# Mixture-of-experts slots of 256 and 128 rows in place of 256-row slots only

## What is computed

```
x = x + tanh(g_xattn[0]) * L0_xattn(layernorm(x), ctx, ctx)
x = x + tanh(g_ffn[0])   * L0_ffn(layernorm(x))
x = x + tanh(g_xattn[1]) * L1_xattn(ctx, layernorm(x), mask)
x = x + tanh(g_ffn[1])   * L1_ffn(layernorm(x))

def L1_ffn(x):                     # 4096 x 256, float32
    probs = softmax(x @ gate_w + gate_b)          # 8 experts
    top_w, top_idx = top_k(probs, 2); top_w = top_w / sum(top_w)
    h = silu(x @ w1[e]) * (x @ w3[e])             # 256 -> 1024, for each expert e
    out_e = h @ w2[e]                             # 1024 -> 256
    return sum over e of combine[token, e] * out_e
```

## Time and profile before

| | |
|---|---|
| median of 3 runs | 2118.34 us (2112.92 to 2119.6) |
| the profiled execution | 2116.76 us, span from first to last instruction 2115.0 us |
| PE busy over the span | 1902.5 us (90%) |
| DVE busy | 1563.4 us (74%) |
| ACT busy | 1156.6 us (55%) |
| POOL busy | 921.6 us (44%) |
| mean granted PE clock | 0.954 of 2.4 GHz |

### The profile page before, as it was taken

The page is one execution under the profiler, slowest core; times in us unless marked ns, Lnnn a source line. Parts: engine busy times, 40 slices in busy tenths (PEclk is TensorE's granted clock), DMA queues, the critical chain, the costliest instruction groups (busy, mean ns, idle before and its releaser), DMA issues. The chain is left out here.

```text
span 2115.0 us, 36023 instructions
## 1 busy us (share of the span) xinstructions
PE 1902.5 (90%) x11968; PEld 1329.2 (63%) x11968; DVE 1563.4 (74%) x3233; ACT 1156.6 (55%) x2414; POOL 921.6 (44%) x683
## 2 busy tenths in 40 slices
PE   5899999986669999998999999929999999999998
PEld 2566666665223434343434343419999999999998
DVE  7999999993466677776767778547777777777775
ACT  2356665655335555655555655515555666666663
POOL 6999999981633334352434331112222222222222
PEclk8899999998679999999999999959999999999999
DMA  5222222210425151524242441037666666666661
GB/s 172 111 91 111 88 111 111 84 58 1 112 57 123 31 125 60 112 66 105 78 100 91 89 118 34 31 104 254 223 223 217 217 226 228 226 230 226 220 213 60
DMA packets 140067, 271.47 MB, mean 128 GB/s; under 512 B 13915, under 2 KB 91823, under 8 KB 134066
## 3 DMA queue, kind: packets, MB, share of 16 engines
q1 hardware_dynamic: 128812, 244.55, 37.6%
q0 software_dynamic: 10624, 25.26, 3.2%
q10 hardware_dynamic: 518, 0.27, 0.0%
HBM read 201.96 MB, written 71.39 MB: 129 GB/s over the span
## 5 line engine op out<-in xcount | busy, mean ns | idle before, releaser
L1447 DVE CUSTOM_DVE_ANT_0 x_dump<-x_ps,x_bias_q 128x512 bf16<-128x512 f32 x512 | 353.0, 689 | 103.5 <-PE x_ps L1140 90.4
L1316 ACT ACTIVATE x_PT<-x_ps 128x512 f32<-128x512 f32 x512 | 292.2, 601 | 231.5 <-PE x_ps L1155 228.7
L1929 ACT ACTIVATE X<-m_ps 128x256 f32<-128x256 f32 x312 | 119.1, 382 | 226.0 <-PE m_ps L1866 226.0
L1833 POOL DMA_INDIRECT out_dram<-e_y,e_label x78 | 78.9, 1011 | 362.5 <-DVE e_y L1985 350.6
L1140 PE MATMUL x_ps<-x_KS,x_QS 96*128 96x512 bf16 x512 | 200.7, 393 | 26.2 <-DVE x_mx L1447 25.7
L1154 PE MATMUL x_ps<-x_bias_k,x_ident_b 128*128 128x512 bf16 x512 | 196.8, 384 | 2.2 <-issue 1.1
L1155 PE MATMUL x_ps<-x_QS,x_KS 98*128 98x512 bf16 x512 | 196.5, 384 | 0.0
L1968 DVE TENSOR_TENSOR X<-X,m_ps 128x256 f32<-128x256 f32 x312 | 120.5, 416 | 97.0 <-ACT X L1929 92.5
L1866 PE MATMUL m_ps<-e_x_lo,m_hi 128*128 128x256 f32 x640 | 181.3, 283 | 1.5 <-DVE e_x_lo L1953 1.5
L1866 PE MATMUL m_ps<-e_x_hi,m_hi 128*128 128x256 f32 x640 | 180.9, 283 | 0.0
L1866 PE MATMUL m_ps<-e_x_hi,m_lo 128*128 128x256 f32 x640 | 180.7, 282 | 0.0
(11 more groups left out here) (309 smaller groups left out, 5462.9 us busy)
## 6 DMA issues: line engine op xcount, KB each, us to landing
m_raw<-in_L_ffn_w_dram SPq DMA_DIRECT2D x117, 1024.0 KB, 5.2
expert_in<-a_blank SPq DMA_DIRECT2D x34, 1032.0 KB, 4.3
parts<-x_part SPq DMA_DIRECT2D x24, 512.0 KB, 3.8
m_x<-expert_in SPq DMA_DIRECT2D x39, 258.0 KB, 4.8
next_mask_k<-in_maskT_dram SPq DMA_DIRECT2D x32, 256.0 KB, 2.6
next_mask_q<-in_mask_dram SPq DMA_DIRECT2D x29, 256.0 KB, 2.8
x_KS<-parts SPq DMA_DIRECT2D x16, 384.0 KB, 11.0
x_QS<-parts SPq DMA_DIRECT2D x8, 576.0 KB, 6.4
```

Of the source, the lines that this page charges most:

```text
L1316: act.activation(PT[unit % 2][:, k, :], ps_st[e % 3], ACT.Exp, scale=DH ** -0.5).then_inc(exp_done, 1)
L1447: dve.tensor_tensor_reduce(out=dump[:, :], in0=ps_max[m % 2], in1=bias_q[b % 2][:, q, :], scale=1.0, scalar=NEG, op0=ALU.add, op1=ALU.max, ...
L1929: act.activation(silu[f % 2], ps_h[f % 4][:, 0:BLK], ACT.Silu).then_inc(silu_done, 1)
```

## The change

There are still 39 slots, in another mix: 32 of 256 rows and 7 of 128. The order repeats after 10 slots (`ROUND`), of which the fifth and the tenth (`HALVES`) are small, so slots 4, 9, 14, 19, 24, 29 and 34. An expert's rows are cut into blocks of 256, and a rest of up to 128 rows goes to a small slot; a rest above that to a large one. The table of slots becomes two tables, one for each size, where large slots that are left over take small blocks that found no small slot; working it out takes more instructions.

A small slot loads 129 KB of rows and the same three weight arrays. It has 2 transposes instead of 4; in `hidden` the same 96 matmuls, but with 128 moving columns instead of 256; in `project` 24 matmuls instead of 48; one fetch and one store instead of two; and ACT's and DVE's work on rows is half as wide. Its splitting of weights for the next slot is as before. The slots are written out for slots 0 to 9, for the body of a loop with two turns (10 slots each), and for the last nine.

```diff
+FULL = T * TOPK // BLK
+HALF = NE - 1
+NBLK = FULL + HALF
+ROUND = 10
+HALVES = (4, 9)
...
+def tiles_in(q):
+    return 1 if q % ROUND in HALVES else BT
...
@@ experts: load_rows
-            sp.dma_start(xb[p][:, :, :], xs[bass.ds(at, BLK), :].rearrange("(n p) d -> p n d", p=P)).then_inc(x_in[p], 16)
+            sp.dma_start(xb[p][:, 0:tiles, :], xs[bass.ds(at, tiles * P), :].rearrange("(n p) d -> p n d", p=P)).then_inc(x_in[p], 16)
@@ route, gpsimd
-                pool.iota(starts_i[:, :, :], pattern=[[BLK, NBLK], [0, NE]], base=0, channel_multiplier=0).then_inc(iotas, 1)
+                pool.iota(where_i[:, 0, 0:FULL], pattern=[[BLK, FULL]], base=0, channel_multiplier=0).then_inc(iotas, 1)
+                pool.iota(where_i[:, 0, FULL:], pattern=[[P, HALF]], base=FULL * BLK, channel_multiplier=0).then_inc(iotas, 1)
+                pool.iota(where_i[:, 1, 0:FULL], pattern=[[P, FULL]], base=-FULL * P, channel_multiplier=0).then_inc(iotas, 1)
+                pool.iota(where_i[:, 1, FULL:], pattern=[[P, HALF]], base=0, channel_multiplier=0).then_inc(iotas, 1)
@@ route, vector: 22 instructions in a chain become 36
+                dve.wait_ge(iotas, 4)
+                do(dve.tensor_copy(where[:, :, :], where_i[:, :, :]))
                 do(dve.tensor_tensor(total[:, :], routing.ends_at[0:1, :], routing.region[0:1, :], ALU.subtract))
...
+                do(dve.tensor_tensor(past[:, :, :, :], limit[:, :, :].unsqueeze(3).broadcast_to([1, 2, NBLK, NE]), wide(now), ALU.is_ge))
...
@@ tensor: hidden
-                                mm = three_passes(ps_h[f % 4][:, at:at + BLK],
+                                mm = three_passes(ps_h[f % 4][:, at:at + wide],
                                                   [w[p][n][:, c, f * P:(f + 1) * P] for w in (w_hi, w_lo)],
-                                                  [x_hi[p][:, c, :], x_lo[p][:, c, :]], c == 0, c == KC - 1)
+                                                  [x_hi[p][:, c, 0:wide], x_lo[p][:, c, 0:wide]], c == 0, c == KC - 1)
@@ tensor: project
-                        for n in range(BT):
+                        for n in range(tiles):
...
+                for q in range(ROUND):
+                    hidden(0, q)
+                    turn(0, q + 1)
+                    project(0, q)
+                with pe.Fori(1, ROUNDS) as i:
+                    for q in range(ROUND):
+                        hidden(i, q)
+                        turn(i, q + 1)
+                        project(i, q)
```

More of the change, by code:

```diff
@@ new lines, in _ @@
+                do(dve.tensor_scalar(over[:, :], now[:, 0, NE - 1:NE], float(FULL * BLK), None, ALU.subtract))
+                do(dve.tensor_scalar(more[:, :], over[:, :], 0.0, None, ALU.max))
+                do(dve.tensor_scalar(less[:, :], over[:, :], -0.5, None, ALU.mult))
+                do(dve.tensor_copy(limit[:, 0, :], where[:, 0, :]))
+                do(dve.tensor_scalar(limit[:, 1, :], where[:, 1, :], less[:, 0:1], None, ALU.add))
+                do(dve.tensor_scalar(less[:, :], less[:, :], 0.0, None, ALU.max))
@@ new lines, in _ @@
+                do(dve.tensor_scalar(limit[:, 1, FULL:], where[:, 1, FULL:], less[:, 0:1], more[:, 0:1], ALU.add, ALU.subtract))
+                do(dve.tensor_scalar(weight[:, 0, :], size[:, 0, :], -1.0, None, ALU.mult))
+                do(dve.tensor_tensor(weight[:, 1, 0:NE - 1], size[:, 0, 1:NE], size[:, 0, 0:NE - 1], ALU.subtract))
+                do(dve.tensor_scalar(weight[:, 1, NE - 1:NE], size[:, 0, NE - 1:NE], -1.0, None, ALU.mult))
+                wide = lambda a: a[:, :, :].unsqueeze(2).broadcast_to([1, 2, NBLK, NE])
@@ L1867, in three_passes, with hidden @@
                     return mm
-                def hidden(j, i, p):
+                def hidden(i, q):
+                    j, p, wide = at_slot(i, q), q % 2, tiles_in(q) * P
                     for n in range(2):
@@ L1909, in _ @@
-                hidden(LAST, LAST // 2, 0)
-                project(LAST, LAST // 2, 0)
+                                mm.then_inc(y_ps, BT // tiles)
+                turn(0, 0)
+                for q in range(ROUND):
+                    hidden(0, q)
+                    turn(0, q + 1)
+                    project(0, q)
+                with pe.Fori(1, ROUNDS) as i:
+                    for q in range(ROUND):
+                        hidden(i, q)
+                        turn(i, q + 1)
+                        project(i, q)
@@ L1912, in _, with x_high @@
+                for q in REST:
+                    hidden(ROUNDS, q)
+                    if q + 1 in REST:
+                        turn(ROUNDS, q + 1)
+                    project(ROUNDS, q)
             @block.scalar
             def _(act):
-                def x_high(j, i, p):
-                    act.wait_ge(x_used[p], i + 1)
-                    act.activation(x_hi[p][:, :, :].rearrange("p c n -> p (c n)"), ps_x[p], ACT.Copy).then_inc(x_hi_done, 1)
-                def gated_high(j, k):
+                def x_high(i, q):
+                    p, wide = q % 2, tiles_in(q) * P
+                    act.wait_ge(x_used[p], ROUND // 2 * i + q // 2 + 1)
+                    act.activation(x_hi[p][:, :, 0:wide], ps_x[p].rearrange("p (c n) -> p c n", c=KC)[:, :, 0:wide], ACT.Copy)\
+                        .then_inc(x_hi_done, 1)
@@ L1946, in _ @@
-                hidden(LAST, 0, False)
+                    gated_high(j, FC // 2 - 1, wide)
+                x_high(0, 0)
+                for q in range(ROUND):
+                    hidden(0, q)
+                    x_high(0, q + 1)
+                with act.Fori(1, ROUNDS) as i:
+                    for q in range(ROUND):
+                        hidden(i, q)
+                        x_high(i, q + 1)
+                for q in REST:
+                    hidden(ROUNDS, q, q + 1 in REST)
+                    if q + 1 in REST:
+                        x_high(ROUNDS, q + 1)
@@ L1962, in gate @@
+                def gate(i, q, following=True):
+                    j, p, wide = at_slot(i, q), q % 2, tiles_in(q) * P
                     for k in range(FC // 2):
@@ L2007, in _, with slot @@
-                add_y(LAST, 0)
+                                                 op0=ALU.mult, op1=ALU.add).then_inc(y_left, BT // tiles)
+                def slot(i, q):
+                    gate(i, q)
+                    x_low(i, q + 1)
+                    low_part(dve, at_slot(i, q) + 1, 1 - q % 2, 2)
+                    add_y(i, q)
+                x_low(0, 0)
+                for q in range(ROUND):
+                    slot(0, q)
+                with dve.Fori(1, ROUNDS) as i:
+                    for q in range(ROUND):
+                        slot(i, q)
@@ L2010, in layers @@
+                for q in REST:
+                    if q + 1 in REST:
+                        slot(ROUNDS, q)
+                gate(ROUNDS, len(REST) - 1, False)
+                add_y(ROUNDS, len(REST) - 1)
 def layers(nc, x, ctxT, mask, maskT, g_xattn, g_ffn, L0, F0, L1, M1, out):
```

242 lines of the change are left out of this document (111 added, 131 removed).

## The result

| | before | after |
|---|---|---|
| median | 2119.34 us (2112.92 to 2119.6, 5 runs) | 2101.01 us (2097.69 to 2107.98, 5 runs) |
| the profiled execution | 2116.76 us, span 2115.0 | 2105.28 us, span 2103.5 |
| PE busy | 1902.5 us (90%) | 1879.4 us (89%) |
| start of the routing iota to the end of the span | 715.3 us | 700.5 us |

The changed kernel is faster by 0.7%: the ratio of the times is 0.9928, with a 95% interval of 0.9904 to 0.9952. Forecast were 2100 us, measured 2101.0. A number that comes out so close can still be made of errors that cancel, and here it is: that it lies within 1 us is luck.

The account below looks back on a forecast made before the run. PE was taken to bound every slot. Seven small slots at 3.2 us each (-22.5 us) and the table (+5.1 us) took 2116.8 us to 2099.4, stated as 2100 us; range 2084 to 2108 us, with the fast case.

Parts of the forecast that it names:

- The case of the sum: Whole kernel: the gains and costs of the parts add up as priced, giving 2100 us; chance 72%.
- What bounds the kernel: Experts' slots: PE alone decides, at 17.36 us a slot, until another engine fills the shorter slot.
- Part 1: `project` of a small slot: 24 matmuls fewer save 2.79 us; two fewer transposes save 0.22 us.
- Part 2: `hidden` of a small slot: weight loads bind at 0.114 us a matmul, gaining 0.41 us; ends 0 and 1.1.
- Part 3: Work for the next slot coming late in a small slot: 0.2 us lost, ends 0 and 0.8; no other engine full.
- Part 4: Slot table before the experts: its longer chain, hidden by nothing, costs 5.1 us (4.4 to 6.2).
- Part 5: Loop ends, a store and fetch less in small slots, and the tail: all priced at nothing.
- the fast case: `hidden` of small slots: narrow matmuls pace well below 0.1 us, DVE's 12.1 us bound the slot; 2085 us; chance 12%.
- The slow case: `hidden` of small slots: narrow float32r falls back to the plain price, 0.214 us a matmul; 2165 us; chance 11%.
- a gain handed back: Small slots' neighbours: late row work or weights leave 0.5 us gain a slot instead of 3.2; 2118 us; chance 5%.

Follow-up runs that it names:

- body4: Kernel before the change, with only PE's loop made longer: 9 turns of 4 slots instead of 18 turns of 2; 2117.00 us, ratio 0.9997.
- body6: Kernel before the change, with only PE's loop made longer: 6 turns of 6 slots instead of 18 turns of 2; 2132.77 us, ratio 1.0075.
- bf16 kernel: Changed kernel with both operands of `hidden` in small slots read as bf16, the upper halves of the float32r words; 2113.87 us.

## Why the prediction was right

The sum was 2116.8 - 22.5 + 5.1 = 2099.4 us, so 17.4 us less for the experts. Measured are 14 to 15 less. The case of the sum is the one that came; one of its terms, the loop's return, was wrongly at nothing. By parts:

- **What bounds the kernel**: right. The chain runs over PE in every slot, small or large, and the large ones keep their length (`hidden` 11.39 and 11.31 us).
- **Part 1**: right. Turn and half `project` take 3.30 us, 3.22 were forecast. The gain is 2.71 us instead of 2.79, with 0.21 for the transposes ahead of the slot.
- **Part 2**: the mechanism is right, the load binds; the pace was 0.111 us, between the ends of 0.107 and 0.118, and 0.003 under the value taken. 0.68 us gained, 0.41 forecast. It lies midway between its two neighbours, the transposes' 0.107 and L1203's 0.114. (The "eight matmuls" of L1203 are eight records of four, for a plain f32 matmul has two records here; the pace of a load stays.)
- **Part 3**: right that nothing becomes late. DVE's rows at the end of the small slot (remainders, then `x_low`) answer:

```profile
1516.90 0.99 DVE L2042 TENSOR_TENSOR e_g_lo<-X,e_g_hi 128x256 fp32r<-128x256 f32 x2
...
1517.95 0.69 DVE L2017 TENSOR_TENSOR e_x_lo<-m_ps,e_x_hi 128x512 fp32r<-128x512 f32 x1
```

  `x_low` ends at 1518.64, 0.6 us ahead of the next `hidden` at 1519.23, where the prediction had 0.4; the stall that it allowed, 0.2 us, was 0. Parts 1 to 3 together gave 3.60 us a slot instead of 3.2, so 25.2 instead of 22.5.
- **Part 4**: right in kind, 0.9 us too dear: +4.2 instead of +5.1. The chain was priced at 3.9 us more and took 4.2 more; the wait for the iotas was priced at 1.2 and took 0.47, for a short iota is done in 0.15 us where the one of before had 0.51. From the first iota to the chain's end it is 10.65 us instead of 6.0, +4.6; of these 4.2 reached PE's start in this execution and 3.65 in the second (+4.3 by the means above).
- **Part 5**: here a step failed. "The new code has two turns of a long body" was written as a reason for nothing, and it was a cost: 6.8 us in the one return (7.3 in the second execution), nearly half of the 14.8 that the experts gained net. The evenness over the short returns was carried over to a return of another body; `body4` and `body6` show, with nothing else changed, that a return is free at 592 matmuls and costs at 888, and the queues show why: the longer body's code has to be loaded again. That it was of the dearer kind goes, by the rows, with the small slot (19) at the body's end; no run tested that.
- **What the sum left out**: everything ahead of the experts was taken as equal. It is the same code, but its end, which is the start of the iota, came at 1403.03 us in this profiled execution and at 1395.25 in the second one of the same kernel; over the executions of the changed kernel and its variants it lies between 1395.25 and 1408.19, and in the three with the table of before at 1399.74, 1400.22 and 1399.31.

This last point decides how the nearness of 2100 and 2101 is to be read. The experts gained 14 to 15 us, not 17.4, and the medians 18.3; so, by subtraction, some 3.5 us came from ahead of the experts. The traces, one execution each, don't show this gain: over the eleven of the changed kernel and its variants the iota starts at 1399.6 us on the mean, over the three others at 1399.8. So the forecast's change was 1 us off the measured one because 2.7 us more from the small slots, 0.9 less for the table, 6.8 for the return and these 3.5 nearly cancel, and the base of the sum, 2116.8 us, was 2.5 under before's later median; that is luck. The windows (as above) of the same 100 us show what goes with it, first in the second execution of the changed kernel, then in the first:

```profile
860.00:960.00 100.00, 93.72 (x503) 40.49 (x502) 71.50 (x247) 57.81 (x121) 41.05 (x41) 1.00 0.36 92
```
```profile
860.00:960.00 100.00, 94.56 (x484) 40.99 (x485) 69.16 (x238) 55.58 (x117) 39.00 (x39) 0.97 0.35 85
```

Where the granted clock is 0.97, fewer matmuls are through in the same time (484 instead of 503). Why the clock falls in one execution and not in another, and whether the changed kernel truly has the better draw, no run here settles. A spread of 13 us ahead of the experts is also wide enough to hide the 7 us of the written-out loops, which can be seen in every stretch and in no median.

Of the rivals, the fast case fell for float32r (0.111 us at 128 and at 192 columns). The floor of 12.1 us that it named is DVE's work for a small slot, but the work need not lie within the slot: in the bf16 kernel DVE had 2.5 us to spare in 12.21. The slow case, two records at the plain price, would have shown at 128 columns and didn't. Of a gain handed back there was nothing in the small slots: the stall was 0. The bf16 kernel shows that this rival is real once PE gets faster.

## What to carry to other kernels

Halving the moving columns of a matmul halves its time only as long as the columns bind; where each matmul loads 128 new float32r columns, the floor is the load, and a smaller block pays only in the stages where whole matmuls go away (here `project`, 2.71 of 3.60 us a slot, for half of the rows). Before a loop's body is made longer, count its return as a cost until a trace shows that it is none, on the engine that sets the end above all: write that engine's loop out, or keep its body short, and look in the DMA queues for packets of instructions. By the rows, not by a test, a long body had better end with a slot that keeps the engine busy for long. And compare stretches between fixed points of the traces besides the medians: a cost of 7 us was plain in the one and absent in the other.

## What the runs showed of the hardware that was not expected

- A `hidden` of 64 moving columns dropped the granted clock from 1.00 to 0.50 in the middle of an unbroken row of float32r pairs; 128 and 192 columns did not. Making matmuls smaller where the load binds can so make them slower: 16.2 us instead of 10.7. At that clock the pairs stand 0.21 us apart, so the load's pace follows the clock too.
- bf16 pairs of load and matmul at 128 columns start 0.057 us apart, float32r pairs 0.111.
- A loop's return on PE costs nothing at a body of 592 matmuls, and a gap of 1.5 to 4.6 us at bodies of 888 to 1480, in which 16 KB of PE's code are loaded; the next matmul starts 1.6 to 1.8 us after the load. Behind gaps of over 4 us, and four of the six of 2.0 to 2.5, the clock is lower for a while, which costs 1.5 to 2.9 us more; behind the other two and the one of 1.5 us it costs 0.1.
- Indirect DMAs are issued by POOL in about 1 us, unless they begin while DVE runs `low_part`, whose two inputs both lie in SBUF. Then they end 0.9 to 1.0 us after the `low_part`, however long that takes (16 of 17 in the changed kernel, up to 2.95 us). Those that begin up to 1 us before a `low_part` take 1.0 to 1.3 us, though they run beside it. Two fetches that follow each other, and DVE beside the second:

```profile
1528.28 1.05 POOL L1880 DMA_INDIRECT e_y<-out_dram,e_label  x1 [5.08 <-issue]
1529.64 2.89 POOL L1880 DMA_INDIRECT e_y<-out_dram,e_label  x1 [0.31 <-issue]
```
```profile
1529.36 2.29 DVE L1727 TENSOR_TENSOR m_lo<-m_raw,m_hi 128x2048 fp32r<-128x2048 f32 x1
```

  The second ends at 1532.53, about 0.9 us after `low_part` (1531.65). With three `low_part` in a row it was 6.47 us, above. The Trainium skill, page "GPSIMD Engine Reference", section "Key points", has POOL's SBUF interfaces shared with VectorE, with contention from DVE instructions that have two SBUF inputs; these rows agree with it. In the kernel with 192 columns the same shows at the end of a loop that feeds itself, add to store to fetch to the next add: DVE waited 5.91 us for fetched rows, and POOL's store behind it took 2.83 us.

```profile
1892.96 0.88 DVE L2051 SCALAR_TENSOR_TENSOR e_y<-m_ps,e_label,e_y 128x256 f32<-128x256 f32 x2 [5.91 <-DMA e_y<-out_dram,e_label]
```
```profile
1894.75 2.83 POOL L1888 DMA_INDIRECT out_dram<-e_y,e_label  x1 [6.82 <-DVE e_y L2051]
```

  In the changed kernel DVE's waits for fetched rows sum to 8.7 us and never reached PE; in this one they did. That was seen, not tested.
